# Gate value product moved into the late feature steps, tanh of receptance read by ScalarE from PSUM

## The reference, cut to what matters

```python
# attention with Fourier features, 16 heads of 16 channels, 128 frequencies
x2 = layernorm(xn) * g + b
q, k, v = x2 @ wq + bq, x2 @ wk + bk, x2 @ wv + bv
phi(y) = concat([cos(y @ proj / 4), sin(y @ proj / 4)]) / sqrt(128)
kv   = einsum('blhm,blhd->bhmd', phi(k), v)
attn = einsum('blhm,bhmd->blhd', phi(q), kv) @ wo + bo
s    = xn + attn;  s = s + relu(layernorm(s) @ w1 + b1) @ w2 + b2
# gate, on time-mixed inputs (x_prev is xn one token earlier)
xr, xk = mu_r * xn + (1 - mu_r) * x_prev, mu_k * xn + (1 - mu_k) * x_prev
out = sigmoid(xr @ W_r) * (square(relu(xk @ W_k)) @ W_v)
x = x + s * silu(out)
```

## Time and profile before

| | us |
|---|---|
| runs of the kernel, three | 2205.34 median (2202.84 to 2207.92) |
| the profiled execution | 2196.74 |
| its span in the trace | 2195.0 |
| first stage in it | about 836 of the span |
| PE / DVE / ACT / POOL busy in the span | 1872.7 / 1670.2 / 1264.9 / 1217.7 |

### The profile page before, as it was taken

The page is one execution under the profiler, slowest core; times in us unless marked ns, Lnnn a source line. Parts: engine busy times, 40 slices in busy tenths (PEclk is TensorE's granted clock), DMA queues, the critical chain, the costliest instruction groups (busy, mean ns, idle before and its releaser), DMA issues. The chain is left out here.

```text
span 2195.0 us, 26582 instructions
## 1 busy us (share of the span) xinstructions
PE 1872.7 (85%) x8596; PEld 1061.4 (48%) x8596; DVE 1670.2 (76%) x2189; ACT 1264.9 (58%) x1685; POOL 1217.7 (55%) x651
## 2 busy tenths in 40 slices
PE   5689988998998898789879898999885677998996
PEld 3345545654654463233334332533242235887885
DVE  4874797497579525899999999999989995232787
ACT  4864874576477414666655665466544334665774
POOL 2701810350180002688888999989976674222576
PEclk9999999999999999999999999999999989999998
DMA  7420641443054106898899899988899984223453
GB/s 202 98 57 15 140 101 53 115 96 98 23 131 97 77 24 52 279 316 292 272 314 315 264 275 301 305 296 284 285 300 363 328 322 148 99 97 100 139 160 105
DMA packets 177321, 402.68 MB, mean 183 GB/s; under 512 B 48174, under 2 KB 77104, under 8 KB 176034
## 3 DMA queue, kind: packets, MB, share of 16 engines
q1 hardware_dynamic: 165154, 371.09, 54.7%
q0 software_dynamic: 12032, 29.90, 4.7%
HBM read 356.30 MB, written 45.51 MB: 183 GB/s over the span
## 5 line engine op out<-in xcount | busy, mean ns | idle before, releaser
L1336 POOL TENSOR_TENSOR late<-late,rows 128x1024 f32<-128x1024 f32 x256 | 603.3, 2365 | 147.9 <-DVE late L1816 141.4
L1987 PE MATMUL m_Q<-late,ident_m 128*128 128x512 f32 x1024 | 529.4, 649 | 152.7 <-POOL late L1336 115.0
L1816 DVE TENSOR_TENSOR_SCAN late<-m_Q,late 128x1024 f32<-128x1024 f32 x256 | 586.3, 2290 | 45.1 <-ACT m_Q L1522 17.0
L1522 ACT ACTIVATE m_Q<-late,acol 128x1024 f32<-128x1024 f32 x256 | 286.0, 1117 | 363.2 <-DVE late L1816 361.7
L1987 PEld LDWEIGHTS m_Q<-late,ident_m 128*128 128x128 f32 x1024 | 195.9, 203 | 452.4 <-POOL late L1336 251.3
L1809 DVE TENSOR_TENSOR late<-m_Q,rows 128x1024 f32<-128x1024 f32 x256 | 307.0, 1199 | 13.3 <-DMA rows<-bc_s 13.2
L553 DVE SCALAR_TENSOR_TENSOR early<-early,work 128x1024 f32<-128x1024 f32 x128 | 155.9, 1218 | 44.8 <-ACT early L699 42.9
L2050 PE MATMUL m_Q<-late 128*128 128x128 f32 x1248 | 158.9, 281 | 8.9 <-issue 1.3
L2050 PEld LDWEIGHTS m_Q<-late 128*128 128x128 f32 x1248 | 147.1, 194 | 36.3 <-issue 35.0
L709 ACT ACTIVATE early<-early 128x1024 f32<-128x1024 f32 x128 | 135.2, 1056 | 29.9 <-DVE early L558 29.0
L710 ACT ACTIVATE early<-early,halfpi 128x1024 f32<-128x1024 f32 x128 | 145.8, 1139 | 0.0
(11 more groups left out here) (243 smaller groups left out, 3344.3 us busy)
## 6 DMA issues: line engine op xcount, KB each, us to landing
rows<-bc_s SPq DMA_DIRECT2D x512, 512.0 KB, 5.8
rows<-st_s SPq DMA_DIRECT2D x64, 384.0 KB, 5.8
r_s<-late SPq DMA_DIRECT2D x39, 256.0 KB, 2.0
rows<-st_s SPq DMA_DIRECT2D x64, 128.0 KB, 6.4
st_s<-early SPq DMA_DIRECT2D x8, 768.0 KB, 5.4
xin<-in_x SPq DMA_DIRECT2D x4, 1024.0 KB, 5.7
xres<-in_x SPq DMA_DIRECT2D x4, 1024.0 KB, 5.6
mx_s<-s SPq DMA_DIRECT2D x4, 1024.0 KB, 4.5
```

The costliest lines, as they stand in the source:

```text
L1336: nc.gpsimd.tensor_tensor(pr[:, n % NH, :], h[:, n % NH, :], cb[:, n % NCB, :], ALU.mult).then_inc(pr_ok, 1)
L1522: A(dA[:, :], dt[:, (b * KI + m) % 2, :], ACT.Exp, scale=acol[:, m, i % NS:i % NS + 1]).then_inc(dA_ok, 1)
L1816: v_.tensor_tensor_scan(h[:, n % NH, :], dA[:, :], dB[:, n % 2, :], 0.0, ALU.mult, ALU.add).then_inc(h_ok, 1)
L1987: ins = mm(half(Y, c), ident[:, :], half(pr[:, n % NH, :], c), start=False, stop=(n % NS == NS - 1), skip_group_check=True)
```

## The change

`vv` leaves the tail: its halves now stand in steps 26/27 and 28/29 (job 0 and 1), and ACT copies it to `xr` within steps 26 and 28. Keys come first (`kk` at 16 and 18, taken by DVE at 18 and 20), receptance at 20 and 22. DVE no longer copies receptance: ACT takes the tanh straight from PSUM into `v`, in steps 20 and 22, ahead of that step's sines. The transposes `xn` move from steps 24 and 26 to 24 and 25, with ACT's copy between the two sines; `gl` moves from 28 to 30, and `gate` from step 30 to behind the loop. DVE's product reads `v` in place of `kr`. What SP and POOL execute keeps its order.

```diff
-AMID = {16: ("kk", 0), 18: ("r", 0), 20: ("r", 1), 22: ("kk", 1)}
-TAKEN = {18: ("kk", 0), 20: ("r", 0), 22: ("r", 1), 24: ("kk", 1)}
+AMID = {16: ("kk", 0), 18: ("kk", 1), 20: ("r", 0), 22: ("r", 1), 26: ("vv", 0), 28: ("vv", 1)}
+TAKEN = {18: ("kk", 0), 20: ("kk", 1)}
-PREVIOUS = {24: ("xn", 0), 26: ("xn", 1), 28: ("gl",), 30: ("gate",)}
+PREVIOUS = {24: ("xn", 0), 25: ("xn", 1), 30: ("gl",)}
...
+    if b:
+        jobs.append((b - 1, ("gate",)))
-    rest = [("wo", i) for i in range(2)] + [("vv", i) for i in range(2)] + [("xf", c) for c in range(NC_)]
+    rest = [("wo", i) for i in range(2)] + [("xf", c) for c in range(NC_)]
...
# VectorE
-                            if kind == "r":
-                                dv.wait_ge(feat_used, b * 32 + 16)
-                                v_.tensor_copy(four(v, i), slot(b, kind, i)[:, :]).then_inc(r_ok, 1)
-                            else:
-                                v_.tensor_scalar(kr[:, i, :], slot(b, kind, i)[:, :], 0.0, None, ALU.max).then_inc(kr_ok, 1)
+                            v_.tensor_scalar(kr[:, i, :], slot(b, kind, i)[:, :], 0.0, None, ALU.max).then_inc(kr_ok, 1)
...
+                    evac_attention(b, 2)
+                    evac_attention(b, 3)
                     if b:
                         gate_logits(b - 1)
-                    evac_attention(b, 2)
-                    evac_attention(b, 3)
...
-                        dv.wait_ge(th_ok, b * 2 + i + 1)
-                        v_.scalar_tensor_tensor(four(gt, i), four(gt, i), 1.0, xr[:, i, :], ALU.add, ALU.mult).then_inc(out_ok, 1)
+                        dv.wait_ge(r_ok, b * 2 + i + 1)
+                        v_.scalar_tensor_tensor(four(gt, i), four(v, i), 1.0, xr[:, i, :], ALU.add, ALU.mult).then_inc(out_ok, 1)
...
# ScalarE
+                        if s in AMID and AMID[s][0] != "kk":
+                            kind, i = AMID[s]
+                            wait_full(ac, b, kind, i)
+                            if kind == "r":
+                                ac.wait_ge(feat_used, b * 32 + 16)
+                                A(four(v, i), slot(b, kind, i)[:, :], ACT.Tanh, scale=0.5).then_inc(r_ok, 1)
+                            else:
+                                A(xr[:, i, :], slot(b, kind, i)[:, :], ACT.Identity).then_inc(vv_ok, 1)
                         ac.wait_ge(ra_ok, b * 32 + s + 1)
                         A(fs[:, s % NF_, :], fs[:, s % NF_, :], ACT.Sin, scale=-TURN).then_inc(feat_ok, 1)
+                        if b and s in (24, 25):
+                            normed(b - 1, s - 24)
                         A(fc[:, s % NF_, :], fc[:, s % NF_, :], ACT.Sin, scale=-TURN, bias=halfpi[:, :]).then_inc(feat_ok, 1)
-                        if b and s in (24, 26):
-                            normed(b - 1, (s - 24) // 2)
-                        elif b and s == 28:
+                        if b and s == 30:
                             logits(b - 1)
-                    for i in range(2):
-                        wait_full(ac, b, "vv", i)
-                        A(xr[:, i, :], slot(b, "vv", i)[:, :], ACT.Identity).then_inc(vv_ok, 1)
-                    ac.wait_ge(kact_ok, b * KD + KD)
-                    for i in range(2):
-                        ac.wait_ge(r_ok, b * 2 + i + 1)
-                        A(four(gt, i), four(v, i), ACT.Tanh, scale=0.5).then_inc(th_ok, 1)
...
# TensorE
+                        elif kind == "vv":
+                            pe.wait_ge(kact_ok, b * KD + KD)
+                            by_token(b, ("vv", i), tokens_of(xk, i), wvv, pieces=(2, 3) if second else (0, 1))
...
+                    if b:
+                        logits_turned(b - 1)
                     pe.wait_ge(at_ok, b * 4 + 4)
                     for i in range(2):
                         by_token(b, ("wo", i), tokens_of(aT, i), wo)
-                    pe.wait_ge(kact_ok, b * KD + KD)
-                    for i in range(2):
-                        by_token(b, ("vv", i), tokens_of(xk, i), wvv)
```

More of the change, by code:

```diff
@@ L168, in phase_a @@
         kv_ok = sem("kv_ok"); kvs_ok = sem("kvs_ok"); kv_turned = sem("kv_turned"); at_ok = sem("at_ok")
-        h_ok = sem("h_ok"); mix_ok = sem("mix_ok"); part_ok = sem("mix_parts"); th_ok = sem("th_ok")
+        h_ok = sem("h_ok"); mix_ok = sem("mix_ok"); part_ok = sem("mix_parts");
         kr_ok = sem("kr_ok"); kact_ok = sem("kact_ok"); out_ok = sem("out_ok"); g_ok = sem("g_ok")
@@ L960, in batch @@
                         if b and s in PREVIOUS:
-                            if s in (24, 26):
-                                normed(b - 1, (s - 24) // 2)
-                            elif s == 28:
+                            if s in (24, 25):
+                                normed(b - 1, s - 24)
+                            else:
                                 logits(b - 1)
-                            else:
-                                logits_turned(b - 1)
+                    if b:
+                        logits_turned(b - 1)
                     pe.wait_ge(at_ok, b * 4 + 4)
```

## The result

| | before | changed |
|---|---|---|
| median of the runs, us | 2202.84 (7 runs, 2190.21 to 2208.27) | 2216.02 (7 runs, 2210.79 to 2220.23) |
| ratio, 95% interval | | 1.007 (1.0048 to 1.0092) |
| profiled execution | 2196.74, span 2195.0 | 2218.96, span 2217.2 |

The change makes the kernel slower, by 0.7%. Forecast were 2218 and a sum of +12.8 us; the medians differ by 13.2.

The account below looks back on a forecast made before the run. PE, DVE and ACT hand work round in the features with little slack; the tail is a chain. Terms 4.9 + 7.0 + 0.9 = 12.8 us on 2205.3 gave 2218 us, range 2203 to 2230.

Parts of the forecast that it names:

- Late features, batches 1 to 3: From step 20 to output product `wo`: ACT waits for PE's halves, `wo` starts 1.6 us later per batch, 4.9 total.
- T: Clock zero: end of DVE's evacuation in step 20 (receptance before, keys in the changed kernel).
- Late features, batch 0: Same stretch in batch 0: two tanh, two copies, four table loads (three unhidden) put `wo` 7.0 us later.
- Rival 3: Much slower: half clock falls into PE's halves inside the features, which ACT waits for; 2229 us, chance 15%.
- The tail: From `wo` through the hidden layer: earlier x2T copy against half clock after PE's 7.3 us idle; +0.9 us over four batches.
- the term of 16.5 us for the hidden layer: In each tail the hidden layer starts half-clocked and takes 16.5 us, bounds 14.0 and 17.4; +3.8 us over four batches.
- a granted clock under 0.9 over L820 in every batch: Sign in the tail's hidden layer; the forecast would be wrong if L820 ran at 1.00.
- A second term: Duration of `wo` itself: taken as unchanged, with bounds of -1.5 and +1.5 us for each batch.
- Rival 1: Faster: PE's halves are always there in time, so ACT does not wait in the features; 2195 us, chance 12%.
- rival 2: No change: PE keeps its full clock in the tail, hidden layers take 14.0 us; about 2204 us, chance 12%.

Follow-up runs that it names:

- e2_vv_back: Changed kernel with the value product and its copy put back in the tail, behind the output product: 2190.93 us, ratio to before 0.9975.
- e1_tanh_back: Changed kernel with only its tanh part undone (DVE copies receptance again, ACT takes the tanh in the tail): 2221.75 us, ratio to before 1.0127.
- e3_warm: Changed kernel with one small silu ahead of ACT's first copy, loading the function tables once at the start: 2209.63 us, ratio to before 1.0068.
- e8_fill: Changed kernel with 13 idle matmuls between output product and transposes in the tail: 2218.52 us, ratio to before 1.011.
- e10_fill7: Changed kernel with 7 idle matmuls between output product and transposes in the tail: 2204.41 us, ratio to before 1.0051.
- e7_before_split: Kernel before the change, with POOL's addition of the output bias to xn cut in four pieces: 2194.22 us, ratio to before 0.9989.
- e13_changed: Changed kernel measured again without any edit: 2215.90 us against 2196.91 for the kernel before, ratio 1.0092.

## Why the prediction was right

Forecast +12.8 us, measured +13.2 between the medians. By its steps, from the two traces:

**Late features, batches 1 to 3: mechanism and times right, size 0.8 short.** From T, the forecast put the end of the first tanh at 6.5, the start of the `vv` copy at 27.9 and the end of the last sines at 45.9; the rows give 6.5 (510.97 + 1.02), 27.9 (533.34) and 45.8 (550.16 + 1.13). `wo` was to come at 47.85 and came at 48.7. The rest is the last attend: it ran at half clock, 1.90 in place of 1.07, after 2.04 us in which PE stood for the sines. So +2.4 in place of +1.6 a batch. L556 of step 20 came out at 1.95, not 2.5. That the loss is the value product's and not the tanh's, e2_vv_back and e1_tanh_back show; the prediction had the waits in steps 26 and 28 but blamed both edits alike, and there the runs correct it: in batches 1 to 3 the tanh's wait of 1.8 us costs less than DVE's copy did, and only in batch 0 is the tanh a loss.

**Late features, batch 0: +10.5 in place of +7.0.** The loads stand where they were put: the first hides in the wait (tanh at 117.56, PE done then), the three others do not. e3_warm prices them at 3.5 to 4.6 us, forecast 3.8. The step that was short is PE's: an attend and the first half of `vv` 0 ran at half clock (PE's timeline of the changed kernel, batch 0),

```profile
130.78 1.18 PE L924 MATMUL atp<-early,kv 128*32 128x256 f32 x16 [2.79 <-ACT early L718]
...
133.76 1.94 PE L924 MATMUL atp<-early,kv 128*32 128x256 f32 x16 [0.84 <-ACT early L718]
135.63 3.36 PE L783 MATMUL work<-wvv,rows 128*128 128x256 f32 x8
```

3.36 us in place of 1.97, and 1.94 in place of 1.07, behind gaps of 2.79 and 0.84; in e3_warm, without the loads, the same half takes 1.99. The second half of `vv` 0 so ended at T+30.3 and not at T+27.9: 2.4 of the 3.5 us that were missing. Another 1.0 is ACT standing for DVE ahead of the last sines, which the forecast had not. Rival 3 had named half clock in a half that ACT waits for, and it happened in one batch out of four.

**The tail: sign wrong, +0.9 forecast, -4.4 measured.** `wo` to the end of the hidden layer took 38.1, 35.7, 32.4 and 35.8 us before and 34.1, 34.1, 34.6 and 34.9 after. The idle gap was 7.3 as forecast, the transposes did run at half clock (granted 0.50), and first transpose to hidden layer is 3.51, forecast 3.55. What failed is the term of 16.5 us for the hidden layer: 14.4 to 14.7, at a granted 0.97 to 0.95. The four layers were to lose 3.8 us and won 4.1. With it failed one of the signs that the prediction named, a granted clock under 0.9 over L820 in every batch. The clock was back 0.9 to 1.4 us behind the layer's start; before, in batch 0, it had stood at 0.50 for the layer's first 5.6 us. I put that down to the transposes, which fill 3.5 us without a gap now that they run slowly, so that part of the half-clocked stretch lies in them; no run tests this by itself. I had taken the layer's row of lowest clock, 16.78, which had stood behind 3.0 us of idle PE. e8_fill and e10_fill7 show that the gap is the cause of what is left: filled, the layer takes 14.0. A second term was put at nothing and was not: `wo` took 8.86, 8.85, 9.21 and 9.39 us where it had 8.69, 8.71, 7.17 and 8.81, 2.9 more in all, and 2.0 of that in batch 2 alone, over the bound of 1.5; the last attend ahead of it stood 2.04 us for the sines and both ran at half clock for a while.

**What no step had.** From the end of the hidden layer before (in batch 0, from the start) up to T, batches 0 to 3 took 0.9, 1.6, 4.4 and -0.3 us more than before, 6.6 in all. The 4.4 are the stretch of e7_before_split: DVE's sign clearing meets POOL's addition or misses it, by tenths of a microsecond. The kernel before shows the slow form too, in batch 3 (59.1 from the start of the features to the key product, against 54.3), and e13_changed in batch 1 alone. The 1.6 are something else, a key product at half clock, behind PE's wait for DVE's evacuation of the keys before. PE's timeline of the changed kernel, batch 1 and then batch 2, where it did not happen:

```profile
298.67 3.57 PE L772 MATMUL work<-rows,wkk 128*128 128x512 f32 x4 [2.31 <-DVE kr L544]
...
497.65 1.96 PE L772 MATMUL work<-rows,wkk 128*128 128x512 f32 x4 [2.26 <-DVE kr L544]
```

It comes back in batches 2 and 3 of e13_changed (3.25 and 3.51 us). With 2 us in the second stage, whose instructions are the same, these 6.6 make up what the profiled executions differ by beyond the sum's own terms, which came to 2.4 x 3 + 10.5 - 4.4 = 13.3. How much of the 6.6 is scatter and how much belongs to the change, the runs do not settle; the 19.0 us between the medians of e13_changed speak for a part of it. So the total of 12.8 was right by luck: two errors of more than 5 us met, the features were short by 5.9 and the tail too high by 5.3.

Rival 1 (ACT does not wait) fell by the four waits in front of L711 and L713; rival 2 (full clock in the tail) by the granted 0.50, though in the hidden layer it was closer than my forecast.

The page "ScalarE: Activation LUTs" of the Trainium skill, section "Rules for kernel authors", is borne out in its rule (group by table set): e3_warm takes 3.5 to 4.6 us off batch 0. Its figure of about 2.7 us for a switch is not: an `ACT_TABLE_LOAD` takes 1.28 here, and the sine behind the load at 118.60 starts 1.30 us after the load does. The Trainium skill's page "SBUF — State Buffer", section "SBUF: two separate sides", says that DVE and POOL share a pair of ports that one of them holds for a whole instruction. The rows agree in both directions: L556 took 4.64 beside POOL's addition, and in the tail it was POOL that took 6.56.

## What to carry to other kernels

A product that fills an idle engine in the tail is free; moved among steps in which three engines hand banks round, it costs not only its own time but a wait in its reader, and here reading it one step later moved the wait to the writer. Look at who frees a PSUM bank and how far down that engine's list the reading stands: here the tanh from PSUM gained 3 us in each of three batches, and lost 3 in the first one even with its tables loaded. Load function tables once, with a function whose set serves all the others. And before explaining a few microseconds between two profiles, look for a pair of operations that may or may not collide.

## What the runs showed of the hardware

- POOL's addition (4.54 us) holds up DVE's 128 x 1024 sign clearing (0.69 alone) until it is done: 4.64. Cut in four, it lets DVE in between the pieces: 1.38 and 1.49. In reverse, DVE's two products hold up POOL's addition from 4.52 to 6.56.
- A 128 x 512 float32 matmul with its weights takes 0.87 us as issued here (two records in the trace; 13 in 11.32), at the full clock.
- After a gap of 7.3 us PE's transposes ran at half clock for 3.5 us, and the clock was back 0.9 to 1.4 us into the dense work behind them; with the gap cut to 1.26 by idle matmuls, transposes (1.10 and 1.09 for eight) and hidden layer (14.00) ran at the full clock.
- The silu's tables serve sine, tanh, relu and identity as well: in e3_warm one load stands at the start, and no other follows in the first stage.
